# A two-layer transformer kernel on one core: the second router's work is split and moved, the gather and the giving back are reordered

## The reference, cut to what matters

```python
logits = x @ router_w.T                      # 2048 tokens, 8 experts
probs = jax.nn.softmax(logits, axis=-1)
top_p, top_i = jax.lax.top_k(probs, K)       # K = 2
expert_flat = top_i.T.reshape(-1)            # all first picks, then all second picks
...
pos = jnp.take_along_axis(jnp.cumsum(onehot, axis=0), expert_flat[:, None], axis=1)[:, 0] - 1
keep = pos < CAP                             # CAP = 64
dest = expert_flat * CAP + pos
...
buf = jnp.zeros((E * CAP, H), x.dtype).at[dest_m].set(x[token_idx], mode='drop')
h = jax.nn.gelu(buf @ w1.T + b1, approximate=False) @ w2.T + b2
gathered = jnp.where(keep[:, None], h[jnp.where(keep, dest, 0)], 0.0) * probs_flat[:, None]
out = jnp.zeros_like(x).at[token_idx].add(gathered)
```

## Time and profile before

| what | us |
|---|---|
| median of 3 runs (lowest to highest) | 928.34 (925.98 to 932.94) |
| the profiled execution, its own time | 935.09 |
| its span, first to last instruction | 933.3 |
| PE, DVE, ACT, POOL busy | 839.0, 698.6, 495.8, 391.7 |
| mean granted TensorE clock, share of 2.4 GHz | 0.954 |

### The profile page before, as it was taken

One profiled execution on the slowest core, in us unless ns is written; L12 is line 12 of the kernel. 1 busy time (PEld: TensorE's weight loads), 2 busy tenths in 40 slices (PEclk: granted clock), 3 DMA queues, 4 the chain that ended last, 5 costly groups with the idle time before them and its releaser, 6 DMA issues.

```text
span 933.3 us, 22064 instructions
## 1 busy us (share of the span) xinstructions
PE 839.0 (90%) x8221; PEld 519.7 (56%) x8221; DVE 698.6 (75%) x1932; ACT 495.8 (53%) x1176; POOL 391.7 (42%) x735
## 2 busy tenths in 40 slices
PE   5899999997598989879999999999999999994895
PEld 2455555553344444445655776666767766673465
DVE  3677777776667877758989888888888888835536
ACT  3477777764334445337666556555555565522053
POOL 4446565543444745433433333333333333342534
PEclk8899999999788989999999999999999999997798
DMA  7333332320000000005667565656555655520402
GB/s 261 109 93 79 73 79 60 93 31 7 1 1 1 1 1 0 1 1 100 123 115 117 99 112 95 107 97 94 97 97 100 111 94 108 105 53 1 91 1 91
DMA packets 218458, 67.70 MB, mean 73 GB/s; under 512 B 211296, under 2 KB 214384, under 8 KB 218224
## 3 DMA queue, kind: packets, MB, share of 16 engines
q1 hardware_dynamic: 218352, 66.29, 35.8%
HBM read 17.92 MB, written 4.19 MB: 24 GB/s over the span
## 4 chain that ended last, share of the span: by engine, by line
PE 62%; DVE 12%; issue 10%; POOL 7%; DMA 5%; ACT 2%; SPq 1%; POOLq 0%; DVEq 0%; ACTq 0%
PE bank L446 12%; PE bank L447 11%; PE bank L448 11%; DMA att<-w_lo 4%; PE bank L573 4%; PE bank L801 3%; PE bank L803 3%; PE bank L802 3%; DVE nm L1365 3%; PE bank L520 2%; POOL scr L1891 2%; DVE w_lo L1389 2%; PE bank L515 2%; POOL scr L1896 2%; PE bank L496 2%
## 5 line engine op out<-in xcount | busy, mean ns | idle before, releaser
L1103 ACT ACTIVATE att<-att,nm 128x512 f32<-128x512 f32 (+3 forms) x256 | 141.5, 553 | 104.0 <-DVE nm L1378 102.6
L1008 ACT ACTIVATE scr<-bank 128x512 bf16<-128x512 f32 (+3 forms) x210 | 111.5, 550 | 112.6 <-PE bank L803 49.9
L446 PE MATMUL bank<-w_hi,scr 128*128 128x256 bf16 (+1 forms) x480 | 148.1, 309 | 10.7 <-DVE scr L1307 10.0
L447 PE MATMUL bank<-w_lo,scr 128*128 128x256 bf16 (+1 forms) x480 | 148.0, 308 | 0.0
L448 PE MATMUL bank<-w_hi,scr 128*128 128x256 bf16 (+1 forms) x480 | 147.8, 308 | 0.0
L1365 DVE TENSOR_REDUCE nm<-bank 128x1 f32<-128x512 f32 (+3 forms) x256 | 110.6, 484 | 40.1 <-PE bank L520 40.1
L1378 DVE CUSTOM_DVE_ANT_0 att<-bank,consts 128x512 f32<-128x512 f32 (+3 forms) x256 | 113.4, 483 | 15.0 <-PE bank L448 15.0
L1940 POOL TENSOR_SCALAR wqkv_hi<-att,rr 128x512 bf16<-128x512 f32 (+3 forms) x128 | 65.6, 532 | 138.6 <-DVE rr L1395 138.6
L1307 DVE TENSOR_TENSOR scr<-bank,scr 128x256 bf16<-128x256 f32 (+1 forms) x146 | 77.4, 540 | 58.2 <-ACT scr L1008 58.0
L1054 ACT ACTIVATE att<-bank 128x512 f32<-128x512 f32 (+1 forms) x192 | 90.8, 528 | 52.8 <-PE bank L557 52.6
L1940 POOL TENSOR_SCALAR w_hi<-att,rr 128x512 bf16<-128x512 f32 (+3 forms) x128 | 65.6, 532 | 106.5 <-DVE rr L1395 106.5
(11 more groups left out here) (206 smaller groups left out, 2060.8 us busy)
## 6 DMA issues: line engine op xcount, KB each, us to landing
scr<-wall_in SPq DMA_DIRECT2D x19, 512.0 KB, 4.7
x_tok<-x_tok_in SPq DMA_DIRECT2D x1, 2048.0 KB, 10.5
v_by_token<-scr SPq DMA_DIRECT2D x16, 128.0 KB, 1.8
scr<-v_by_token SPq DMA_DIRECT2D x16, 128.0 KB, 3.3
scr<-x_t_in SPq DMA_DIRECT2D x3, 512.0 KB, 5.9
out<-x_tok SPq DMA_DIRECT2D x3, 512.0 KB, 2.6
scr<-wqkv_in SPq DMA_DIRECT2D x2, 384.0 KB, 3.7
att<-w_hi SPq DMA_TRANSPOSE x32, 3.3
```

Source lines behind the costliest of these rows:

```text
L446: pe.matmul(out, l_hi, r_hi, start=start, stop=False, skip_group_check=check)
L447: pe.matmul(out, l_hi, r_lo, start=False, stop=False, skip_group_check=check)
L1008: return act.activation(out, in_, ACT.Copy)
L1103: last = act.activation(at, at, ACT.Exp, bias=nm[:, j % 2, qt:qt + 1], scale=-1.0, accum_out=rs[:, j % 2, qt:qt + 1])
```

## The change

It has six parts, none of which changes what is computed (sums of the same numbers are partly taken in another order).

1. In the first mixture's routing steps DVE does `joined(n - 2, 2)` ahead of `route`, and the low part of "cm" ahead of `choose_first`.
2. PE computes heads 0 to 11 of tile 12 inside the last group, and the rest of the dense products in another order: first 12 heads of tile 14, then 13 of tile 13 and of tile 15, then the remaining heads.
3. The last router runs for tiles 0 to 11 between the logits of tile 11 and the low part of the last context, and for tiles 12 to 15 alone at the end (`route_tiles`). The first pick is taken from the logits, the second from the exponentials without their sum; the sum, its reciprocal and the largest exponential come in behind the one-hots.
4. The counts are made otherwise: the picks are summed by two products, ACT copies the sums to bf16, and three products with masks made beforehand add the counts of earlier tiles. DVE makes three masks and a table of limits for this.
5. `gather(k, t)` goes through all tiles for one half of the features and then for the other. The low part of the last block of rows moves from POOL to DVE, between the eighth and the ninth one-hot; the gates come behind all one-hots.
6. The first four tiles are given back in two passes. Five tiles (`SHARED`) are scaled out of PSUM by ACT and added by POOL. DVE adds the other eleven and measures all 16 in the order of `MEASURES`. POOL makes the deviations of 4, 4, 4, 2, 1 and 1 tiles, ACT norms the first 14, DVE the last two.

The core of the diff:

```diff
+SHARED = (1, 4, 7, 10, 13)
+JOINED = (0, 2, 3, 5, 6, 8, 9, 11, 12, 14, 15)
+MEASURES = (0, 2, 3, 1, 5, 6, 4, 8, 7, 9, 11, 10, 12, 14, 13, 15)
+DEVIATIONS = ((0, 4), (4, 4), (8, 4), (12, 2), (14, 1), (15, 1))
...
+                    if is_last(g) and j >= 2:
+                        if j == 2:
+                            pe.wait_ge(c["plo"], NH)
+                        last_dense(DONE, 6 * (j - 2), 6 * (j - 1))
                     if behind >= 2:
                         l1_pv(*((g, j - 2) if j >= 2 else (g - 1, j + 2)))
...
                 pe.wait_ge(e["picks"], 2)
-                pe.matmul(bank[7][:, 0:2 * NT * NX], upper_b[:, :], picks[:, :, :], start=True, stop=False)
-                for n in range(2 * NT - 1):
...
+                for k in range(2):
+                    last = pe.matmul(bank[5][:, k * P:(k + 1) * P], picks[:, k * NT:(k + 1) * NT, :], ones_b[:, :],
+                                     start=True, stop=True)
+                last.then_inc(e["cnt"], 1)
...
+                pe.wait_ge(e["cntb"], 1)
+                pe.matmul(rank[:, 0:P], count_b[:, 0:P], past_b, start=False, stop=False, skip_group_check=True)
...
+            pe.wait_ge(c["max"], 3 * NH)
+            last_dense(DONE + 2, 0, 12)
             l1_pv(NT - 1, 2)
-            pe.wait_ge(c["plo"], NH)
-            last_dense(DONE, 0, HEADS - 2)
             hold(pe, c["kvl"], 2 * NT)
+            last_dense(DONE + 1, 0, 13)
             last_turn(DONE - 1)
-            pe.wait_ge(c["max"], 3 * NH)
-            last_dense(DONE + 1, 0, HEADS - 2)
+            last_dense(DONE + 3, 0, 13)
             last_logits(DONE - 1)
             iota_rows()
-            last_dense(DONE + 2, 0, HEADS - 2)
             l1_pv(NT - 1, 3)
-            last_dense(DONE + 3, 0, HEADS - 2)
...
-            for t in range(NT):
-                gather(t)
+            for k in range(KE):
+                for t in range(NT):
+                    gather(k, t)
...
+            for parts in (0, 1), (2, 3):
+                for t in range(TT):
+                    give_back(t, parts)
+            for t in range(TT, NT):
+                give_back(t, range(TT))
...
+            share(1)
+            share(4)
+            norms(0, 4)
+            share(7)
+            share(10)
+            norms(4, 4)
+            share(13)
+            norms(8, 4)
+            norms(12, 2)
...
+                if 0 <= n - 2:
+                    joined(n - 2, 2)
                 routed = 0 <= n + 4 < NT and (n + 4) % TT == TT - 1
                 if routed:
                     route((n + 4) // TT)
...
+                if 0 <= behind < NT:
+                    turned_low("cm", behind)
                 if routed:
                     choose_first((n + 4) // TT)
-                if 0 <= behind < NT:
-                    turned_low("cm", behind)
...
+                chain(dve.tensor_reduce(r1c[:, 2, ts], lg[:, ts, :], AX.X, ALU.max))
+                dve.tensor_tensor(row(0), lg[:, ts, :], wide(2), ALU.subtract).then_inc(e["lgd"], 1)
+                dve.wait_ge(e["lgd"], turn)
+                chain(dve.scalar_tensor_tensor(row(4), row(0), 0.0, rev[:, ts, :], ALU.is_equal, ALU.mult))
+                chain(dve.tensor_reduce(r1c[:, 2, ts], row(4), AX.X, ALU.max))
+                chain(dve.tensor_tensor(first[:, ts, :], rev[:, ts, :], wide(2), ALU.is_equal))
+                dve.wait_ge(e["ex"], turn)
+                chain(dve.scalar_tensor_tensor(row(3), first[:, ts, :], -2.0, row(1), ALU.mult, ALU.add))
...
+            dve.wait_ge(e["lgc"], DONE)
+            route_tiles(0, DONE, 1)
...
+            add_share(1)
+            add_share(4)
+            deviations(0, 4)
+            add_share(7)
+            add_share(10)
+            deviations(4, 4)
+            add_share(13)
+            for t0, n in DEVIATIONS[2:]:
+                deviations(t0, n)
```

234 lines of the change are left out of this document (145 added, 89 removed).

## The result

| | before | after |
|---|---|---|
| median of 4 runs each (lowest to highest), us | 930.64 (925.98 to 933.54) | 917.57 (915.64 to 919.75) |
| ratio, 95% interval | | 0.985 (0.982 to 0.988) |
| the profiled execution, its own time (span) | 935.09 (933.3) | 918.97 (917.2) |
| mean granted clock | 0.954 | 0.959 |

What follows compares the result with a forecast made beforehand. PE, busy for 90% of the span, was taken as the bound, so gains lie where it stands still: 3.9 + 3.4 + 4.9 + 2.3 + 0.65 + 0.2 - 1.5 = 13.85 us, median 928.34 to 914.5 us, range 906 to 921.

Steps and rivals of the forecast that it cites:

- Part 1: First mixture's routing steps, DVE reordered: steps 3 and 7 win 1.86 us each, step 11 about 0.2; 3.9 us, bounds 0 to 11.7.
- The join of tile n-2: First mixture's routing steps: moved ahead of routing, it fills idle DVE time but meets ScalarE's table loads, so wins nothing.
- The term for the low part: First mixture, steps 3 and 7: low part of cm earlier, DVE's wait for a gelu goes, 1.86 us won each.
- Its sign: Steps 3 and 7: granted clock stays at 1.00, step shrinks by 1.9 us, PE waits at the transposes instead.
- The 0.2 for step 11: First mixture's step 11: about 0.2 us won, since its gelu was hardly late.
- the rival in which it falls: PE's new waits in the step after routing bring the clock down, so routing steps pay nothing: 918.4 us; chance 0.18.
- Part 2: Last group and dense products: added heads fill two PE waits for transposing DMAs; 3.4 us won, 1.5 to 3.6.
- Part 3: Router's picks, from the copy of the logits to the second picks: fewer, smaller DVE instructions; 4.9 us won.
- part 4: Counts between picks and slots: 3.87 us becomes 1.6, 2.3 won; slots behind them 2.45 to 1.8, 0.65 won.
- Part 5: Gather: same 64 products, but one copy and one subtraction at its end where two overlapped; 0.2 us won.
- Part 6: Giving back: DVE does less but waits for POOL, which falls behind; 1.5 us lost, between 1.5 won and 4 lost.
- The rival with the clock held down through the gather: First gather pass never lets the clock up: 926.2 us, or 947 if the FFN stays slow too; chance 0.05.

Runs made afterwards that it cites:

- the run with the join alone: Kernel before with only joined(n-2, 2) moved ahead of mix(n, 0), the low part of cm left in place: 927.37 us, ratio 0.996.
- its own experiment: Kernel before with POOL holding its last subtraction of rows (2.12 us) back until both picks are made: 932.40 us, ratio 0.999.
- the experiments with the order: After with ScalarE's share of tile 7 ahead of norms(0,4) and share of 10 ahead of norms(4,4): 914.22 us, ratio 0.981 against before.
- one pass: After with the first four tiles given back in one pass in place of two: 914.70 us, ratio 0.982 against before.
- both edits of the giving back: After with ScalarE's shares of 7 and 10 ahead of its norms and the first four tiles in one pass: 911.60 us, ratio 0.979 against before.
- The three variants with a late join: After with one-pass giving back and shares before norms, plus joined(n-2,2) late at steps 4, 8, 12; at 12; or at 11: 912.58, 909.65, 912.62 us.
- the join late in three steps: After with one-pass giving back and shares before norms, joined(n-2,2) behind mix(n,0) at n = 4, 8, 12: 912.58 us, ratio 0.978 against before.
- the join late at step 12 alone: After with one-pass giving back and shares before norms, joined(n-2,2) behind mix(n,0) only at n = 12: 909.65 us, ratio 0.978 against before.
- step 11 as before: After with one-pass giving back and shares before norms, both part 1 moves undone at n = 11: 912.62 us, ratio 0.980 against before.

## Why the prediction was right, and where it was not

- **Part 1 (forecast 3.9, measured 6.5 to 7.9 from step 1 to 15).** The step that failed is "The join of tile n-2, moved ahead of the routing, fills an idle place of DVE but meets ScalarE's table loads behind it: nothing". It looked only at the three routing steps, and so does point 1 of the change's description. The line stands outside `if routed` and so acts in every step, as the diff shows. In the other steps it is worth 0.48 to 1.01 us each; the run with the join alone shows it. The term for the low part was right in kind and 0.3 to 0.4 us too high: 1.44 to 1.57 per pair, forecast 1.86. Its sign, step 3 shorter by 1.9, has to be read over the pair: step 3 lost 4.03 us and step 4 gained 2.47. The 0.2 for step 11 was not there: steps 11 and 12 are 0.03 us longer where the clock holds and 1.4 where it falls. PE does wait at the transposes of the next step instead, 3.0 us in pieces, and the clock stays up there, so the rival in which it falls was wrong for steps 4 and 8 and right in some executions for step 12.
- **Part 2 (3.4, measured 3.6).** As worked out: no wait left, the last group full, the routing of twelve tiles under it. Over all traces the stretch from the join of tile 0 in the second attention to that of tile 12 is 3.9 us shorter (mean 315.9 in five with the old tail, 312.0 in nine with the new).
- **Part 3 (4.9, measured 4.94), part 4 (2.3 and 0.65, measured 2.35 and 0.66).** All right. POOL's subtraction made 1.9 of part 3, by its own experiment; the rest is fewer and smaller instructions. (The rows have 16 instructions of 128 elements behind the copy, the one of 2.22 us among them, not 17 and that one; the term stands.) Parts 2 and 4 have no run of their own and rest on the rows of their stages.
- **Part 5 (0.2, one profile 0.64).** Not a gain that can be called shown. From the first one-hot to DVE's first addition, the two-pass start taken off, the traces with the old order have 40.3 to 41.4 us and those with the new 40.1 to 41.4. What spreads them is how long PE stays at half clock in the gather, which differs between executions of one code.
- **Part 6 (+1.5, measured +2.27 at DVE's end, +2.57 at the span's).** The stall before tile 7 was 1.64 us where 1.5 was forecast. A second one, 0.56 us before tile 13, from the same cause a round later, is not named, though the prediction's own times (POOL's addition of 13 at +17.4, DVE free some 0.5 before) leave room for it. That addition ended at +17.90, for POOL had waited 2.62 us for ScalarE's share, and its last deviations came 0.6 to 0.8 us later than worked out. By the experiments with the order and with one pass, all of the loss is order: the sharing itself gains 1.3 to 1.7 us against the traces with the old order.
- The sum was short by 2.3 us on the profiles: 3.3 too little in the mixture and 0.8 in the small terms, against 1.1 too little loss at the end and 0.8 lost in stretches that nothing changed. That it came within 1 us of the 13.07 between the medians is in part luck: the join's gain, 5.3 us in the plain steps that the sum put at nothing, was offset by the loss of clock in step 12, the larger loss at the end and the scatter of the executions. The rival with the clock held down through the gather didn't occur; the gather reached the full clock as before.

Still open is why the clock falls behind some waits of 2.3 to 3.1 us and not behind others; the runs show only that the code doesn't decide it.

A better kernel than both came out: after with both edits of the giving back, 911.6 us and 0.979 of before (after: 0.985; the intervals, 0.974 to 0.984 and 0.982 to 0.988, overlap a little, but DVE ends the stage 3.5 to 3.9 us earlier in all four traces with both edits than in the three with after's code there). The three variants with a late join are the same within their intervals.

## What to carry to other kernels

Where a diff moves a line in a loop, work it out for every iteration, the plain ones first: 0.5 to 1.0 us in each of eight plain steps, 5.3 in all, outweighed the 3.1 won in steps 3, 4, 7 and 8, which looked special. Two engines that each wait for the other's last product must not have the answer queued behind work that itself waits (ACT's share behind norms that need POOL's deviations); put the short instruction that others wait for ahead. And before a long POOL instruction is placed, look at what DVE does beside it: in an idle place of DVE it cost nothing, across its chain it cost its whole length.

## What the runs showed of the hardware that was not expected

- The same wait, with the same code, is followed by the full clock in one execution and by half of it in another. For step 12's wait of 2.65 to 2.70 us the clock fell in three of seven traces (after, the run with ScalarE's order, the join late in three steps) and held in four; each fall costs 1.4 us. Step 11's wait of 2.30 us had none in three traces, but waits of 2.46 and 2.83 us there did, and one of 3.08 us in step 12 had none: the length of the wait alone doesn't decide. The Trainium skill (TensorE: Matmul & The Clock Gate, "What's actually happening") says that the same kernel shows different numbers of slow products from run to run; the traces agree.
- The gather starts at half clock in every kernel looked at, and how long it stays there differs between two of the last kernels, which have the same code behind the mixture. The first with the join late at step 12 alone (first one-hot at 844.63), the second with step 11 as before (848.13):

```profile
850.00:851.00 1.00, 1.00 (x5) 0.35 (x3) 1.00 (x4) 0.00 (x0) 0.00 (x0) 0.72 1.15 224
```

```profile
851.50:852.50 1.00, 1.00 (x6) 0.42 (x5) 1.00 (x2) 0.00 (x0) 0.00 (x0) 0.97 1.15 215
```

The clock rises some 5.9 us behind the first one-hot in the one and 3.4 in the other (the slices' 0.72 and 0.97 are means of both levels), and first one-hot to first addition takes 41.35 and 40.05 us.
